# Memory attention: the row, query and row-score work of a batch made three steps ahead, and the keys turned in the values' PSUM fill

## What is computed

```python
x = x + _L1_xattn_ref(_layernorm(x), ctx_1024, Wq, Wkv, Wc)      # 8 batches, 256 rows, 256 wide
...
qp = q @ Wq.T                                   # queries
scores = qp @ kv^T                              # every row against the 256 rows of the context
idx = argmax(scores, axis=-1)                   # its best context row
mem = kv[idx]                                   # one memory row for each row
mk, mv = split(mem @ Wkv.T)                     # one key and one value of 16, shared by all heads
logits = heads(qp) @ mk^T * scale               # 16 heads of 16
out = softmax(logits) @ mv
```

## Time and profile before

| | us |
|---|---|
| median of 3 runs | 1382.69 (1382.04 to 1382.87) |
| the profiled execution, its own time | 1381.46 |
| its span, first to last instruction | 1379.7 |
| memory_attention, first load to last divide | 920.7 to 1139.7 |
| of it, before the first maximum | 920.7 to 961.2 |

### The profile page before, as it was taken

How to read it: one execution, slowest core, us unless ns; L and a number is a source line. 1 busy time by engine, 2 the same in 40 slices (tenths; PEclk the granted TensorE clock), 3 DMA queues, 4 the chain that set the end, 5 groups by cost and what they waited for, 6 DMA issues and landing times. The chain is left out here.

```text
span 1379.7 us, 26090 instructions
## 1 busy us (share of the span) xinstructions
PE 1068.9 (77%) x9362; PEld 728.5 (53%) x9362; DVE 938.7 (68%) x2598; ACT 611.2 (44%) x1228; POOL 434.6 (32%) x605
## 2 busy tenths in 40 slices
PE   4988778984799401899999999953587774999998
PEld 2655554542688401677877778741243432554554
DVE  5587887983377511788888888833777743777776
ACT  2376666763554001566656666512456560000000
POOL 4267754435166371121111111136343100000010
PEclk9699999998899655999999999985689996999999
DMA  7344345330233326466666665334322211100000
GB/s 207 107 120 103 104 109 154 94 94 6 88 105 128 108 91 252 174 239 213 207 227 231 240 230 207 131 117 125 97 76 79 62 38 57 36 24 31 24 8 16
DMA packets 127396, 164.25 MB, mean 119 GB/s; under 512 B 13075, under 2 KB 106022, under 8 KB 124326
## 3 DMA queue, kind: packets, MB, share of 16 engines
q1 hardware_dynamic: 123686, 153.41, 34.2%
q0 software_dynamic: 3584, 9.18, 2.0%
HBM read 117.01 MB, written 45.35 MB: 118 GB/s over the span
## 5 line engine op out<-in xcount | busy, mean ns | idle before, releaser
L1888 PE MATMUL moe_ps_u<-moe_x_hl,moe_up_hl 128*128 128x256 f16 x1932 | 226.2, 276 | 40.2 <-DVE moe_up_hl L1964 31.7
L1888 PEld LDWEIGHTS moe_ps_u<-moe_x_hl,moe_up_hl 128*128 128x128 f16 x1932 | 184.4, 99 | 82.1 <-DVE moe_up_hl L1964 38.2
L2137 PE MATMUL mix_ps_e<-wr_hl,mix_u_hl 128*128 128x512 f16 x768 | 172.3, 380 | 0.0
L2014 POOL CAST moe_mid_hl<-moe_mid 128x256 f16<-128x256 f32 x161 | 68.6, 426 | 312.9 <-DVE moe_mid L1979 312.9
L1964 DVE SCALAR_TENSOR_TENSOR moe_up_hl<-moe_up_in,moe_up_hl 128x512 f16<-128x512 f32 x161 | 105.2, 687 | 54.2 <-ACT moe_up_hl L1937 54.2
L547 ACT ACTIVATE dec_probs<-dec_ps_t 128x768 f32<-128x768 f32 (+1 forms) x128 | 117.2, 916 | 51.5 <-PE dec_ps_t L446 50.1
L2249 DVE SCALAR_TENSOR_TENSOR mix_acc<-mix_ps_e,mix_shares,mix_acc 128x256 f32<-128x256 f32 x256 | 110.4, 477 | 38.9 <-PE mix_ps_e L2137 38.5
L1937 ACT ACTIVATE moe_up_hl<-moe_up_in 128x512 f16<-128x512 f32 x161 | 99.1, 619 | 61.9 <-DMA moe_up_in<-in_moe_w 61.9
L2137 PEld LDWEIGHTS mix_ps_e<-wr_hl,mix_u_hl 128*128 128x128 f16 x768 | 74.8, 98 | 83.3 <-issue 0.8
L1900 PE MATMUL moe_ps_y<-moe_down_hl,moe_mid_hl 128*128 128x256 f16 x966 | 109.1, 273 | 0.0
L1205 DVE TENSOR_REDUCE mem_neg_m<-mem_ps_s 128x2 f32<-128x512 f32 x128 | 82.3, 686 | 31.4 <-PE mem_ps_s L1049 30.6
(11 more groups left out here) (276 smaller groups left out, 1906.1 us busy)
## 6 DMA issues: line engine op xcount, KB each, us to landing
moe_up_in<-in_moe_w SPq DMA_DIRECT2D x23, 1792.0 KB, 7.3
moe_down_in<-in_moe_w SPq DMA_DIRECT2D x23, 896.0 KB, 4.7
dec_q_dram<-dec_q_hl SPq DMA_DIRECT2D x48, 128.0 KB, 2.2
dec_k_dram<-dec_k_hl SPq DMA_DIRECT2D x48, 128.0 KB, 2.0
dec_q_st<-dec_q_dram SPq DMA_DIRECT2D x64, 96.0 KB, 2.6
dec_k_st<-dec_k_dram SPq DMA_DIRECT2D x64, 96.0 KB, 2.6
xs<-zeros SPq DMA_DIRECT2D x8, 736.0 KB
moe_x_in<-xs SPq DMA_DIRECT2D x23, 256.0 KB, 4.4
```

The lines of the kernel that those rows point to most:

```text
L1888: mm = nc.tensor.matmul(bank[:, m, :], up_hl[t.slot][:, w, m, dc, f * P:(f + 1) * P], x_hl[t.slot][:, x, dc, :], start=(dc == 0 and w == x ...
L2014: nc.gpsimd.tensor_copy(mid_hl[t.slot][:, HI, f, :], mid[:, f, :]).then_inc(mid_hi, 1)
L2137: mm = nc.tensor.matmul(ps_e[fill % RING][:, :, :], u_hl[t.slot][:, r, dc, k * P:(k + 1) * P], wr_hl[:, m, dc, 2 * q:2 * q + 2, :], start= ...
```

## The change

- The turn, projection and row scores of a batch are made in step t for **made = t+3** instead of t+2, in eighths 2, 4 and 6 of PE's order; their high halves on ACT in eighths 2 and 4, their low halves on DVE in eighths 3 and 5, the MAX8 in eighth 7. The index search (best_place_of, split off) and table_row follow in eighths 0 and 1 of the next step, where the batch is new = t+2.
- The keys are turned into the second half of ps_far instead of ps_near. For batches 2 to 7 this stands in eighth 5, behind the matmuls of values(t, 1) and in one fill with them; ACT copies outputs and keys out of that fill one after the other. Batches 0 and 1 have a fill of their own. k_st has three buffers instead of two.
- Sums are made four steps ahead, expert outputs weighed five and gathered six ahead (one more each), so the steps begin at -6. ACT's weighings move from eighths 2, 4, 5, 6 to 1, 3, 6, 7. DVE's statistics move from eighth 1 to 4, normalise from 5 to 6.
- POOL's order becomes take_values, gather, then gather_outputs and root (root first in steps before -2), then add_outputs.
- SP loads the context and the rows of batches 2 to 7 only when the first batch's y has landed, and stores the queries behind the loads of maxima and stacks.

```diff
-        LEAD, TAIL = 5, 2
+        LEAD, TAIL = 6, 2
...
-                for kind, n, at in ((TURN, new, 0), (QUERY, new, 1), (BEST, new, 2), (KEYS, new, 7)):
+                for kind, n, at in ((TURN, made, 2), (QUERY, made, 4), (BEST, made, 6)):
...
+        def keys_at(n):
+            return far[PV, 1, n - 2] if n >= 2 else far[KEYS, 0, n]
+        K_ST = 3
...
-        ps_keys = ps_near[:, 0, 0:P].bitcast(F16)
+        ps_keys = ps_far[:, SEQ:SEQ + P].bitcast(F16)
...
+                sp.wait_ge(y_loaded[0], 16 * 2 * TT)
                 for b in range(2):
                     load_context(b)
...
-                    if within(new):
-                        store_queries(new)
                     if within(nxt):
                         load_m(nxt, 0)
                     if within(new):
                         load_stacks(new, 0)
+                    if within(made):
+                        store_queries(made)
...
                 def turn_keys(n):
-                    pe.wait_ge(near_emptied, near[KEYS, n])
+                    if n < 2 and keys_at(n):
+                        pe.wait_ge(far_emptied, keys_at(n))
...
-                    mm.then_inc(far_filled, 1)
+                    if gr == 1 and within(n + 2):
+                        turn_keys(n + 2)
+                    else:
+                        mm.then_inc(far_filled, 1)
...
-                        if p == 0 and within(new):
-                            turn_rows(new)
-                        if p == 1 and within(new):
-                            project(new)
-                        if p == 2 and within(new):
-                            score_rows(new)
-                        if p == 7 and within(new):
+                        if p == 5 and within(new) and not within(t):
                             turn_keys(new)
+                        if p == 2 and within(made):
+                            turn_rows(made)
+                        if p == 4 and within(made):
+                            project(made)
+                        if p == 6 and within(made):
+                            score_rows(made)
...
-                    nc.scalar.copy(o_t[n % 2][:, gr, :], ps_far[:, 0:SEQ]).then_inc(far_emptied, 1)
+                    ins = nc.scalar.copy(o_t[n % 2][:, gr, :], ps_far[:, 0:SEQ])
+                    if gr == 1 and within(n + 2):
+                        copy_keys(n + 2)
+                    else:
+                        ins.then_inc(far_emptied, 1)
...
+                WEIGHED = {1: (0, 0), 3: (0, 1), 6: (1, 0), 7: (1, 1)}
...
-                        if p in (2, 4, 5, 6) and within(mixed):
-                            weigh(mixed, p // 5, {2: 0, 4: 1, 5: 0, 6: 1}[p])
...
+                        if p == 2 and within(made):
+                            rows_high(made)
+                        if p == 4 and within(made):
+                            queries_high(made)
+                        if p in WEIGHED and within(mixed):
+                            weigh(mixed, *WEIGHED[p])
...
+                        if p == 0 and within(new):
+                            best_place_of(new)
+                        if p == 1 and within(new):
+                            table_row(new)
+                        if p == 3 and within(made):
+                            rows_low(made)
+                        if p == 5 and within(made):
+                            queries_low(made)
+                        if p == 7 and within(made):
+                            best_row_of(made)
+                        if p == 4 and within(summed):
                             statistics(summed)
...
+                        if p == 6 and within(summed):
+                            normalise(summed)
...
-                    nxt, new, summed, mixed, drawn = (t + k for k in range(1, 6))
+                    nxt, new, summed, mixed, drawn = t + 1, t + 2, t + 4, t + 5, t + 6
                     if within(nxt):
                         take_values(nxt)
+                    if within(new):
+                        gather(new)
+                    if within(summed) and t < -2:
+                        root(summed)
                     if within(drawn):
                         gather_outputs(drawn)
-                    if within(summed):
+                    if within(summed) and t >= -2:
                         root(summed)
-                    if within(new):
-                        gather(new)
                     if within(mixed):
                         add_outputs(mixed)
```

More of the change, by code:

```diff
@@ L970, in _ @@
                 for t in STEPS:
-                    nxt, new, summed, older = t + 1, t + 2, t + 3, t - 2
+                    nxt, new, made, summed, older = t + 1, t + 2, t + 3, t + 4, t - 2
                     if within(nxt):
@@ L1040, in scores_ready @@
                     if h == 0:
-                        pe.wait_ge(near_emptied, near[KEYS, n] + 1)
+                        pe.wait_ge(far_emptied, keys_at(n) + 1)
                     if h % HALF < 2:
@@ L1059, in shifted_scores @@
                     row, pair = 64 * (h % 2), h // 2
-                    return nc.tensor.matmul(ps_t[pair % 2][:, h % 2, k * SEQ:(k + 1) * SEQ], k_st[n % 2][row:row + ROWS, k * P:(k + 1) * P],
+                    return nc.tensor.matmul(ps_t[pair % 2][:, h % 2, k * SEQ:(k + 1) * SEQ], k_st[n % K_ST][row:row + ROWS, k * P:(k + 1) * P],
                                             q_st[n % 2][row:row + ROWS, pair, :], start=True, stop=True, tile_position=(row, 0))
@@ L1099, in _ @@
                 for t in STEPS:
-                    nxt, new, old = t + 1, t + 2, t - 1
+                    nxt, new, made, old = t + 1, t + 2, t + 3, t - 1
                     for p in range(PAIRS):
@@ L1155, in copy_keys @@
                 def copy_keys(n):
-                    act.wait_ge(near_filled, near[KEYS, n] + 1)
-                    if n >= 2:
-                        act.wait_ge(t_filled, PAIRS * (n - 1))
-                    nc.scalar.copy(k_st[n % 2][:, :], ps_keys).then_inc(near_emptied, 1)
+                    act.wait_ge(far_filled, keys_at(n) + 1)
+                    if n >= K_ST:
+                        act.wait_ge(t_filled, PAIRS * (n - K_ST + 1))
+                    nc.scalar.copy(k_st[n % K_ST][:, :], ps_keys).then_inc(far_emptied, 1)
+                WEIGHED = {1: (0, 0), 3: (0, 1), 6: (1, 0), 7: (1, 1)}
                 def weigh(n, k, j):
@@ L1167, in _ @@
                 for t in STEPS:
-                    nxt, new, old, mixed = t + 1, t + 2, t - 1, t + 4
+                    nxt, new, made, old, mixed = t + 1, t + 2, t + 3, t - 1, t + 5
                     for p in range(PAIRS):
@@ L1181, in _ @@
                             copy_maxima(nxt, 0)
-                        if p == 0 and within(new):
-                            rows_high(new)
-                        if p == 1 and within(new):
-                            queries_high(new)
-                        if p == 7 and within(new):
-                            copy_keys(new)
+                        if p == 5 and within(new) and not within(t):
+                            copy_keys(new)
+                        if p == 2 and within(made):
[4 more added lines that the diff above has]
+                            weigh(mixed, *WEIGHED[p])
             @block.vector
@@ L1256, in _ @@
                 for t in STEPS:
-                    nxt, new, old, summed = t + 1, t + 2, t - 1, t + 3
+                    nxt, new, made, old, summed = t + 1, t + 2, t + 3, t - 1, t + 4
                     for p in range(PAIRS):
@@ L1282, in gather @@
                         pool.wait_ge(v_done, n - 1)
-                        pool.wait_ge(near_filled, near[KEYS, n - 2] + 1)
+                        pool.wait_ge(far_filled, keys_at(n - 2) + 1)
                     for k in range(TT):
```

22 lines of the change are left out of this document (7 added, 15 removed).

## The result

The changed kernel takes 1358.80 us (median of 5 runs, 1352.51 to 1359.58), the kernel before 1382.69 on the same chip (5 runs, 1378.25 to 1383.81). The ratio is 0.983 (95% interval 0.980 to 0.985): 23.9 us faster.

A forecast was written before the change was run, and what follows sets the result against it. No engine was full: near-product waits bound the steps, a gather chain the lead-in. Terms 6.4 - 1.2 - 2.2 - 14.0 - 4.8 + 0.8 = -15.0 from 1381.46 give 1366.5, plus 1.23 for the median: 1367.7 us, range 1362.5 to 1376.5.

The forecast's parts named there:

- The decoder's 1.56: DVE's idle us in a decoder cross-attention step (16.3 - 14.74), added to DVE's busy time to forecast memory-attention steps.
- Steps 1 to 4: Memory-attention steps with near work: from 83.2 us to three of 17.7 plus one of 16.1, -14.0 us.
- Steps -1 and 0: First memory-attention steps, at low PE clock: to 19.5 and 20.5 us, -1.2 and -2.2; lower bounds 17.6 and 16.6.
- The lead-in: Memory attention before the first maximum: longer, as rows_high waits behind weigh(2) and normalise(2) meets a POOL add, +6.4 us.
- Step 5: Memory-attention step keeping only index search, table row and keys: 20.5 to 15.7 us, -4.8.
- Clock: PE clock in the changed steps: one fall to half clock counted in all, +0.8 us.
- Rival 1: PE's clock falls in each of six steps, in eighths without values: about +6 us, 1374 us; chance 0.17.
- rival 3: PE waits for gathered keys in the values' fill, eighth 5, steps 0 to 5: slower, 1388.7 us; chance 0.05.
- The copy of the keys: ACT's copy out of the values' fill: may delay eighth 6's turned outputs 0.4 us, hidden by DVE; costed at nothing.
- Rival 4: Steps keep their 20.4 us because something other than the near chain paces them: 1380.9 us, no change; chance 0.05.
- Rival 2: Lead-in and first steps gain nothing: y(2) lands late (+2.3), steps -1 and 0 stay (+3.4), 1373.4 us; chance 0.20.
- The signs named for a wrong forecast: DVE idle over 2 us per step, PE waiting in eighth 5, or a lead-in past 50 us.

The follow-up runs named there:

- e10: e8 with the index arithmetic of table_row moved from DVE to POOL: 1356.33 us, ratio 0.981 to the kernel before.
- e11: Changed kernel with eight spare matmuls on PE in eighth 6, ahead of the row scores: 1365.27 us, ratio 0.987 to the kernel before.
- e12: Changed kernel with the maxima of the scores over half of the columns (128 of 256): 1343.52 us, ratio 0.971 to the kernel before.
- e4: Changed kernel with one of three products left out of the decoder cross attention's key and value projections: 1353.44 us, ratio 0.980 to the kernel before.
- e1: The changed kernel run again unaltered, for a second profile: 1356.23 us, ratio 0.980 to the kernel before.
- e8: Changed kernel, in steps before -1 y weighings in eighth 7, and root ahead of the gathers in step -2 too: 1354.48 us, ratio 0.980 to before.
- e7: Changed kernel without SP's wait for the first batch's y before its other loads: 1357.31 us, ratio 0.982 to the kernel before.
- e2: Changed kernel with four spare MAX8 on DVE in eighth 7 of each near step: 1371.47 us, ratio 0.993 to the kernel before.
- e5: Changed kernel with near fills in eighths 2, 3 and 4, each drained in its own eighth: 1387.34 us, ratio 1.003 to the kernel before.
- e6: Changed kernel with the keys turned in a fill of their own in eighth 5: 1359.88 us, ratio 0.984 to the kernel before.
- e9: Changed kernel with e2's four spare MAX8 on DVE plus eight spare matmuls on PE in eighth 1: 1370.38 us, ratio 0.992 to before.

## Why the prediction was wrong

**The step that failed** is "A step then costs DVE's busy time plus what the decoder leaves idle: 16.1 + 1.56 = 17.7 us". It took the new step for a sum over one engine and for waits that the decoder would have too. The waits of the earlier trace rows are gone, as told: in steps 1 to 4 neither PE nor DVE waits for a high or low half; what PE waits for there is DVE's maxima, and the longest wait is 1.07 us in eighth 1. But what is left is no sum over an engine. It is eight eighths, five at the round of scores and maxima, 1.87 us, and three above it by 0.14, 0.32 and 0.72: 14.96 + 1.18 = 16.14, measured 16.12. DVE's near work lies in the round's gaps of 0.58 wherever it fits; e10, e11 and e12 show that the eighths set the length and not an engine's sum. The 1.87 stood in the earlier trace rows; I used it to show that before was slow and not to build the new step. The decoder's 1.56 was in part PE's own work (e4). Steps 1 to 4: -14.0 forecast, 83.2 to 64.5 = -18.7 measured. Step 4 came to the forecast 16.1 by chance: 14.56 + 1.56 has nothing to do with its 16.12.

The waits were also the smaller part of what the change took away. Step 4 of before, cut into the same eighths:

```profile
1067.37:1070.40 3.03, 2.63 (x34) 1.24 (x30) 1.90 (x3) 2.62 (x4) 0.23 (x1) 1.00 0.11 33
1070.40:1073.30 2.90, 2.62 (x24) 1.82 (x24) 2.79 (x8) 1.83 (x4) 0.52 (x2) 1.00 0.01 1
1073.30:1076.72 3.42, 3.03 (x36) 1.82 (x36) 3.35 (x11) 1.54 (x3) 0.40 (x1) 1.00 0.40 115
1076.72:1078.57 1.85, 0.43 (x8) 0.29 (x8) 1.68 (x6) 0.19 (x1) 0.02 (x1) 1.00 0.00 0
1078.57:1080.66 2.09, 1.16 (x14) 0.60 (x10) 1.29 (x3) 1.26 (x2) 1.78 (x2) 0.82 0.12 30
1080.66:1083.49 2.83, 2.83 (x28) 1.03 (x24) 1.93 (x4) 1.40 (x2) 0.17 (x1) 0.53 0.36 105
...
```

Eighths 0 to 2 last 9.35 us, in after 5.72. The busiest engine of each has 2.63, 2.79 and 3.35 us of work, 8.77 of the 9.35: by T2 the gain there is mostly that the near work now stands in eighths with room, and 0.6 us at most is waits in which that engine idles. PE was busy 0.43 us of the 1.85 of eighth 3; then the clock fell, to 0.82 in eighth 4 and 0.53 in eighth 5, which took 2.83. In after eighth 5 takes 1.87 at a clock of 1.00, so about 1 us of the step's 4.3 goes with this fall. These shares are read from the rows; no run changes one of them alone.

**Steps -1 and 0** were mis-sized: -1.2 and -2.2 forecast, -3.3 and -6.3 measured (17.40 and 16.35). I stayed near the present ends because PE's clock is low there, and it is, 0.68 and 0.79. But the round is mostly DVE's: at the low clock an eighth of it takes 2.06 to 2.09 in step -1 instead of 1.87. Both ends were even below my lower bounds of 17.6 and 16.6, which held the 1.56; in e1 step -1 was again (17.10), step 0 was not (17.69).

**The lead-in** went as told, 5.15 us longer against 6.4. In order of time:

```profile
934.55 0.80 DVE L1272 TENSOR_SCALAR mem_h_rows<-mem_sums,mem_mv,mem_rstd 128x256 f32<-128x256 f32 x2 [1.11 <-POOL mem_rstd L1338]
...
941.27 0.51 ACT L1182 ACTIVATE mem_y<-mem_y,shares 128x256 f32<-128x256 f32 x1 [4.54 <-DMA mem_y<-ys,slots]
941.69 0.57 ACT L1162 CAST mem_h_hl<-mem_ps_near 128x512 f16<-128x512 f32 x1
...
961.38 2.66 POOL L1330 TENSOR_TENSOR mem_sums<-mem_sums,mem_y 128x512 f32<-128x512 f32 x2
961.43 2.76 DVE L1272 TENSOR_SCALAR mem_h_rows<-mem_sums,mem_mv,mem_rstd 128x256 f32<-128x256 f32 x2 [0.25 <-POOL mem_rstd L1338]
...
964.11 0.75 DVE L1228 MAX8 mem_best<-mem_ps_near 128x8 f32<-128x256 f32 x2
964.78 1.26 DVE L1222 TENSOR_REDUCE mem_neg_m<-mem_ps_s 128x2 f32<-128x512 f32 x2
```

Normalise ends at 935.35, but rows_high stands on ACT behind the weighing of y(2), which waits for its landing till 941.27; and the later normalise meets a POOL add and takes 2.76 us instead of 0.80, with MAX8 behind it. Both were forecast. e8 takes both away (in it that normalise takes 0.80 again) and wins 4.9 us in the lead-in; it does not part them. e7 prices SP's hold at 0.9 to 1.9.

**Step 5**: -4.8 forecast, -4.2 measured; it is 15.06 in e1 and 16.25 here, where one eighth takes 2.83 at the low clock.

**Clock**: +0.8 forecast, about nothing measured; the one stretch each in steps 5 and 6 that falls was there before. Rival 1 did not come: steps 1 to 4 hold 1.00 with PE busy 14.0 of 16.12. The Trainium skill (TensorE: Matmul & The Clock Gate, "A second HAM failure mode: psum-queue depth-cycling") tells of a kernel in which frequent short PE idles between groups of matmuls made the clock swing. The trace disagrees with it in these steps, where PE idles in most eighths (busy 0.79 of 1.85 us in eighth 1). Falls came in e2's steps 2 to 4, behind an eighth 7 stretched to 3.21, and in one or two of steps 1 to 4 of e5, e6, e9 and e10; why there stays open.

**The keys** (rival 3): PE comes to them at 1057.79 in step 4 and waits for no landing; the second issue began at 1052.07, and the landings came 2.4 to 2.9 us after the start of an issue, so over 2.5 us were to spare. The copy of the keys, put at nothing, holds the turned outputs of eighth 6 up by 0.08 us a step. Rival 4 is refuted by the steps themselves. Rival 2 came in neither half: y(2) had landed by 941.27, no later than forecast, the lead-in was 1.25 us shorter than forecast and not 2.3 longer, and steps -1 and 0 fell by 3.3 and 6.3.

The sum measured by the stage's terms is +5.15 - 3.3 - 6.3 - 18.7 - 4.2 = -27.4 against -15.0; of the 12.4 us between them the steps' arithmetic (-1 to 4) makes 10.9.

The signs named for a wrong forecast all look for a slower kernel, and none came: in steps 1 to 4 DVE idles 0.3 to 1.8 us, PE does not wait for the keys in eighth 5, the lead-in is 45.6 us. A sign for a step shorter than DVE's work and 1.56 was missing.

## What to carry to other kernels

Where two engines hand one pair of buffers to and fro, cut the step at that hand-over and read each interval's length: the step is at least the sum over intervals of the longer of the round (here 1.29 + 0.58) and what one engine has to do in that interval, and a fill that is drained in its own interval adds waits (e5, e6). An engine's sum over the step, even 98% busy, says little: taking 0.4 us of DVE work from an interval at its floor gave nothing, and the same eight matmuls were free in one interval and cost 0.87 us in another. So look first for intervals that are overfilled and for others that have room. Take an idle time over from another stage only when its own cause has been found.

## What the runs showed of the hardware

A step without a fall of the clock repeats within 0.02 us from kernel to kernel (16.11 to 16.13 in 27 steps of six kernels). Falls of PE's clock came at other places in the two profiles of one kernel, and a step with one was about 1 us longer or more: step 5 took 16.25 and 15.06, step 4 of e10 17.08 against 16.12, and step 0, at clocks of 0.79 and 0.71, 16.35 and 17.69. Two normalising instructions on DVE took 0.80 us alone and 2.76 beside a 2.66 us add on POOL, and ended 0.15 us after it; in e1, begun 0.72 us into the add, they took 2.10 and ended 0.16 after it.
